# Attention scores of a graph network laid out by unit, head and node, and node sums by one selector for two heads

## The chip, the cores and the metric

The kernel runs on one core of one Trainium2 chip. The metric is the device time of a run in microseconds; three runs of the kernel before gave 3250.22, 3252.38 and 3263.53, median 3252.38 us.

## The reference

Two layers of a graph attention network (GATv2, two heads) over 3125 nodes of 128 features and 100000 edges sorted by their target node, each followed by a small MLP, then a residual and a layer norm. What matters here is the attention:

```python
xl = (h @ Wl + bl).reshape(n, 2, 128)
xr = (h @ Wr + br).reshape(n, 2, 128)
e = leaky_relu(xl[src] + xr[dst], 0.2)
score = einsum('ehd,hd->eh', e, att)
ex = exp(score - segment_max(score, dst)[dst])
out = segment_sum(xl[src] * (ex / (segment_sum(ex, dst)[dst] + 1e-16)), dst)
```

The kernel writes leaky_relu(z) as a linear part plus a multiple of relu(z). The linear part of the source node is one number per node and head, stored beside the row of the node.

## The kernel before, in words

The edges are cut into 391 units of 256 (K = 2 halves of 128 edges). A unit's targets lie in a window of W = 32 nodes. Two units (M = 2) are a step; a layer has 196 steps (NO; the last holds one unit) and some more for the tail. Each engine has a loop over the steps i written out by hand, in which every stage works on units of a fixed number of steps back; semaphores tie the engines together, and each engine keeps to its written order.

For a unit u the stages are:

- GpSimd gathers the 256 source rows (two indirect DMAs, L984; two heads, each 128 features, a one, and the linear part) into `rows`, a ring of 20 units. It does so for both units of a step after it has seen `z_ready` of the unit six before the first of them: the even unit of three steps back.
- SyncE loads the window's target rows (`xrw`, L1008) and the edges' positions (`relb`, L998, L1000).
- VectorE makes the one-hot matrix `oh` (L1330).
- TensorE's `project` (L1108, L1111) puts z = xl[src] + xr[dst] into a PSUM bank, transposed: four transposes and two bf16 matmuls of 256 columns; the last one increments `z_ready`.
- ScalarE takes the relu (`lz`, L1206). It waits for z and for `score_ready` of the step before.
- TensorE's `score` fills a 128x128 tile whose partitions are half, head and node of the window, its columns 128 edges: the linear part (L1083, four matmuls whose weights are one column of `rows` broadcast to 32 columns, the identity moving), the mask (L1086, two), and the relu part (L1092, four, after a wait for `lz_ready`). Outputs of 32 partitions use a strip of 32 columns of the array each. A float32 matmul of this kind is two matmul instructions with a weight load each. After the last one of a step: `score_ready`.
- ScalarE copies both tiles to `hold_s` (L1284); VectorE takes the smallest value of each partition (L1344), brings the two halves together (L1346, L1348), runs the minimum on over the units (L1352 to L1363) and writes `peak`; ScalarE takes the exponential, one instruction a unit (L1290); TensorE transposes it (L1197); ScalarE copies that to `wgt` (L1218).
- TensorE sums the weighted rows by node (L1181, four float32 matmuls a unit); VectorE adds them to a ring of accumulators (L1434).

In TensorE's step i the order is: sums of step i-6, score of the even unit of step i-1, projection of the even unit of step i, the transposes of the exponentials, score of the odd unit of step i-1, node work, projection of the odd unit of step i. From the minimum on, the units are taken as pairs that are shifted by one (`behind`): the odd unit of one step and the even one of the next.

Every eight steps a tile of 128 nodes is ready. Its node work is spread over the steps after: ScalarE copies nine accumulators to `stg`; TensorE adds up the groups of partitions and lays 32 nodes a group side by side (L1148, 24 instructions for each head, in two steps one after the other), then transposes, projection, MLP and, in the first layer, the next layer's projection (L1120 to L1165).

Of the kernel before, what the change touches and what calls it, by code (L numbers as in the profile page):

```python
# [59 lines left out]
assert NT % UT == 0 and N * UE == 8 * E and RING * 8 == P and K == 2 and RING % M == 0  # L60

def gnn(nc, x, src, dst, ln1_g, ln1_b, Wl, bl, Wr, br, att, gat_b, proj_W, proj_b, ln2_g, ln2_b, W1, b1,
# [9 lines left out]
    with ExitStack() as ctx:  # L73
# [11 lines left out]
        sel = sb("sel", [P, H, 3, W], F32)  # L85
# [97 lines left out]
def setup(nc, sb, sem, ps, wts, given, g):  # L183
# [68 lines left out]
    with nc.Block() as block:  # L252
# [31 lines left out]
        def _(pool):  # L284
# [26 lines left out]
            for t in range(K):  # L311
                for h in range(H):
                    o = t * HW + h * W
                    const(pool.affine_select(out=g["sel"][o:o + W, h, :, :], in_=g["sel"][o:o + W, h, :, :],
                                             compare_op=ALU.not_equal, fill=1.0, base=0, pattern=[[0, 3], [-1, W]],
                                             channel_multiplier=1))
            const(pool.memset(g["sel"][:, :, 0, S:W], 0.0))
            const(pool.memset(g["sel"][:, :, 2, 0:S], 0.0))
# [465 lines left out]
def behind(w):  # L784

    return [u for u in range(w * M - 1, w * M + M - 1) if 0 <= u < NU]

def behind_of(u):  # L790

    return (u + 1) // M

def node_step(t):

    return min(behind_of(t * TILE + 20), NO - 1) + 9

def edge_pass(nc, sb, sem, ps, wts, s, layer):
# [8 lines left out]
    lz_ready = sem("lz_ready")  # L810
    score_ready = sem("score_ready")
    held = sem("held")
    low_ready = sem("low_ready")
    low2_ready = sem("low2_ready")
# [68 lines left out]
    rows = sb("rows", [P, ROWS, K, H, RC], F32)  # L883
# [4 lines left out]
    hold_s = sb("hold_s", [P, 4 * M, P], F32)  # L888
    low = sb("low", [P, M], F32)
    low2 = sb("low2", [HW, M], F32)  # L890
    both = sb("both", [HW, M], F32)
    nxt = sb("nxt", [HW, M], F32)
    peak = sb("peak", [P, 4 * M], F32)
    ex = sb("ex", [P, 2 * M, P], F32)
    wgt = sb("wgt", [P, 2 * M, K * HW], F32)
# [46 lines left out]
    STEPS = NO + 7  # L942
# [32 lines left out]

    with nc.Block() as block:
        @block.gpsimd
        def _(pool):
            for u in range(NU):
                if u >= 3 * M and u % M == 0:  # L980
                    pool.wait_ge(z_ready, u - 3 * M + 1)
                for t in range(K):
                    c = u * K + t
                    pool.indirect_dma_start(rows[:, u % ROWS, t, :, :].rearrange("p h c -> p (h c)"), None,  # L984
# [608 lines left out]
```

## Time and profile before

| | |
|---|---|
| median of the timed runs | 3252.38 us |
| the profiled execution, first to last instruction (span) | 3186.6 us |
| what the median has beyond this span | 65.8 us |
| TensorE matmul busy | 2458.3 us (77%) |
| VectorE, ScalarE, GpSimd busy | 1438.1, 1377.3, 1539.2 us |
| mean granted clock of TensorE | 0.897 |

The page gives no other time of the profiled execution than its span. Busy times of TensorE are from records whose ends are modelled. An idle time in the views is put down to what released the engine; "issue" is a time in which the profile shows nothing that the engine waited for, and "remote" a releaser that it could not place.

### The profile page before, as it was taken

The numbers are of one execution on the slowest core, as the hardware profiler recorded it, in microseconds if no ns is written. First come the engines' busy times: TensorE is split into PE (matmuls) and PEld (weight loads), VectorE is DVE, ScalarE is ACT, GpSimd is POOL, SyncE is SP. The second block draws the span as 40 slices with busy tenths as digits, with TensorE's granted clock in tenths as the row PEclk, the third lists the DMA queues.
The fourth block names the chain that finished last, engine by engine and source line by source line (L and its number), as shares of the span: only waits on it lengthen the run. The fifth ranks groups of instructions, "written<-read, shape, count | busy, mean of one in ns | idle before, by whom it ended". The sixth has DMA issues, their size and how long they took to land. (4 is left out here: it accounts for less than half of the span.)

```text
span 3186.6 us, 87535 instructions
## 1 busy us (share of the span) xinstructions
PE 2458.3 (77%) x29581; PEld 1603.2 (50%) x29581; DVE 1438.1 (45%) x5714; ACT 1377.3 (43%) x3472; POOL 1539.2 (48%) x1664
## 2 busy tenths in 40 slices
PE   4678787878787787777758788777787788878775
PEld 2345555555555555555534455555455555545554
DVE  7334444444444444444543444444444443444444
ACT  4234444444444444444533444444444444444444
POOL 5655454554545454455225544455554454454440
PEclk7798999899989999999958998999999888899887
DMA  5443444444434444444224333343333333343330
GB/s 145 144 110 103 108 109 110 110 109 105 114 108 110 112 109 109 109 113 112 57 81 114 109 103 102 103 111 102 106 109 103 103 106 103 105 110 102 103 101 10
DMA packets 236833, 334.02 MB, mean 105 GB/s; under 512 B 51010, under 2 KB 160490, under 8 KB 236394
## 3 DMA queue, kind: packets, MB, share of 16 engines
q0 software_dynamic: 75072, 208.30, 24.9%
q1 hardware_dynamic: 161322, 120.16, 13.2%
q8 instruction: 240, 3.93, 0.5%
q14 instruction: 199, 1.63, 0.2%
HBM read 308.02 MB, written 20.25 MB: 103 GB/s over the span
## 5 line engine op out<-in xcount | busy, mean ns | idle before, releaser
L984 POOL DMA_INDIRECT rows<-table,src_t x1564 | 1488.2, 952 | 1449.6 <-PE psum L1111 1065.2
L1206 ACT ACTIVATE lz<-psum 128x512 f32<-128x512 f32 x782 | 467.1, 597 | 1632.3 <-DMA table<-row 543.2
L1092 PE MATMUL psum<-lz,att_w 128*32 128x128 f32 x6256 | 525.5, 307 | 315.2 <-issue 279.9
L1108 PE MATMUL psum<-ident,rows 128*128 128x128 f32 x3128 | 572.6, 308 | 71.6 <-issue 36.8
L1434 DVE SCALAR_TENSOR_TENSOR acc<-acc,keep,psum 128x129 f32 x782 | 273.3, 349 | 537.1 <-remote 322.4
L1108 PEld LDWEIGHTS psum<-ident,rows 128*128 128x128 f32 x3128 | 377.4, 154 | 258.2 <-issue 219.2
L1092 PEld LDWEIGHTS psum<-lz,att_w 128*32 128x32 f32 x6256 | 198.9, 113 | 491.9 <-issue 406.2
L1083 PE MATMUL psum<-ident,rows 128*32 128x128 f32 x6256 | 409.7, 302 | 35.1 <-issue 33.5
L1181 PE MATMUL psum<-rows,wgt 128*32 128x129 f32 x6256 | 317.2, 287 | 145.2 <-issue 98.8
L1330 DVE TENSOR_SCALAR oh<-relb,win_col,less 128x256 bf16<-128x256 int16 x782 | 247.6, 362 | 237.0 <-PE psum L1092 82.1
L1111 PE MATMUL psum<-oh,xrw 96*128 96x256 bf16 x1564 | 335.3, 297 | 6.6 <-DVE acc L1434 4.1
L1290 ACT ACTIVATE ex<-hold_s,peak 128x128 f32<-128x128 f32 x782 | 274.7, 405 | 84.7 <-DVE peak L1363 82.9
L1181 PEld LDWEIGHTS psum<-rows,wgt 128*32 128x32 f32 x6256 | 175.3, 111 | 269.1 <-issue 256.8
L1086 PE MATMUL psum<-oh,mask_w 128*64 128x128 bf16 x1564 | 218.8, 252 | 61.5 <-issue 60.0
L1083 PEld LDWEIGHTS psum<-ident,rows 128*32 128x32 f32 x6256 | 189.5, 114 | 136.4 <-issue 135.4
L1086 PEld LDWEIGHTS psum<-oh,mask_w 128*64 128x64 bf16 x1564 | 94.9, 110 | 232.1 <-issue 230.0
L1197 PE MATMUL psum<-ident,ex 128*128 128x128 f32 x782 | 176.7, 313 | 11.4 <-ACT wgt L1218 11.4
L1111 PEld LDWEIGHTS psum<-oh,xrw 96*128 96x128 bf16 x1564 | 167.8, 107 | 24.7 <-issue 8.7
L1344 DVE TENSOR_REDUCE low<-hold_s 128x2 f32<-128x256 f32 x392 | 162.2, 414 | 17.8 <-issue 13.0
L1148 PE MATMUL psum<-stg,sel 128*32 128x129 f32 x2400 | 159.8, 280 | 2.6 <-ACT stg L1301 1.7
L1148 PEld LDWEIGHTS psum<-stg,sel 128*32 128x32 f32 x2400 | 142.3, 111 | 6.4 <-ACT stg L1301 4.3
L1284 ACT COPY hold_s<-psum 128x256 f32<-128x256 f32 x392 | 143.6, 366 | 0.0
(256 smaller groups left out, 2169.5 us busy)
## 6 DMA issues: line engine op xcount, KB each, us to landing
xrw<-xr_split SPq DMA_DIRECT2D x782, 48.0 KB
relb<-rel_d SPq DMA_DIRECT2D x194, 192.0 KB
rows<-table,src_t POOLq DMA_INDIRECT x1564
relb<-cyc_d SPq DMA_DIRECT2D x194, 64.0 KB
xr_split<-split SPq DMA_DIRECT2D x50, 192.0 KB, 1.9
table<-row SPq DMA_DIRECT2D x50, 130.0 KB, 2.1
x_mid<-x SPq DMA_DIRECT2D x25, 64.0 KB
xo<-x_mid SPq DMA_DIRECT2D x25, 64.0 KB
```

Of the source, the lines that this page charges most:

```text
L984: pool.indirect_dma_start(rows[:, u % ROWS, t, :, :].rearrange("p h c -> p (h c)"), None, s["tables"][layer][0:NP, :], bass.IndirectOffset ...
L1083: pe.matmul(out[o:o + W, :], rows[:, u % ROWS, t, h, D + 1:RC].to_broadcast([P, W]), s["ident"][:, :], start=True, stop=False, skip_group_ ...
L1086: pe.matmul(out[t * HW:t * HW + HW, :], s["mask_w"][:, :], oh[:, u % (3 * M), t * P:t * P + P], start=False, stop=False, skip_group_check= ...
L1092: m = pe.matmul(out[o:o + W, :], w["att_w"][:, h * W:h * W + W], lz[:, u % M, h * UE + t * P:h * UE + t * P + P], start=False, stop=True, ...
L1108: pe.matmul(z[:, o:o + P], rows[:, u % ROWS, t, h, 0:D], s["ident"][:, :], is_transpose=True, start=(h == 0 and t == 0), stop=False, skip_ ...
L1111: m = pe.matmul(z[:, h * UE:h * UE + UE], xrw[:, place(u), h * D:h * D + D], oh[0:3 * W, u % (3 * M), :], start=False, stop=(h == H - 1), ...
L1148: mm = pe.matmul(bank(t)[m * W:m * W + W, h * (D + 1):h * (D + 1) + D + 1], s["sel"][:, h, c, :], stg[t % 2][:, 2 * m + c, :], start=(c == 0),
L1181: m = pe.matmul(sum_bank(i - 6)[o:o + W, c:c + D + 1], wgt[:, (u + 1) % (2 * M), o:o + W], rows[:, u % ROWS, t, h, 0:D + 1], start=True, s ...
L1206: act.activation(lz[:, u % M, :], ps[u % M][:, :], ACT.Relu).then_inc(lz_ready, 1)
L1290: m = act.activation(ex[:, (u + 1) % (2 * M), :], hold_s[:, place(u), :], ACT.Exp, bias=peak[:, place(u + 1):place(u + 1) + 1], scale=-1.0)
L1330: m = v.tensor_scalar(oh[:, u % (3 * M), :], relb[:, u % RING, :], s["win_col"][:, 0:1], s["less"][:, 0:1], ALU.is_equal, ALU.subtract)
L1434: m = v.scalar_tensor_tensor(a, a, s["keep"][:, u:u + 1], sum_bank(i - 7)[:, c:c + D + 1], ALU.mult, ALU.add)
```

## The change

A step's scores get one tile for both units. Before, a unit had a tile of its own: partitions were half, head and node, columns 128 edges. Now partitions are unit of the step, head and node (2 x 2 x 32), columns the unit's 256 edges.

- The linear part: ScalarE copies the one column per half, unit and head, broadcast to 32 columns, to a new tile `lin`, for both units at once; TensorE then needs two matmuls of 128 output partitions a step (before: eight of 32). ScalarE does this at the end of its step i for the units of step i, after it has waited for their rows.
- The mask: one matmul of 256 columns a unit (before: two of 128). The relu part: two of 256 columns (before: four of 128).
- `hold_s`, `ex` and `wgt` follow. The exponential is one instruction a step of 128x256 (before: two of 128x128). The minimum: a reduce over 256 columns, one copy of the second unit's 64 partitions; the operation that joined the halves is gone. `peak` is one column a step; the second unit's half is written a step later than the first's.
- The shift by one unit is gone (`behind` becomes `of_step`). Exponential, its transpose, `wgt`, sums and accumulation come one step later than before in the loops, which for the odd unit is the same place, and `node_step` grows by one.
- Node sums: the selector is laid out for both heads, so that a matmul gives 64 output partitions (two heads of 32 nodes): 12 instructions instead of 24 in each of the two steps. The copy to `gT` (L1241) reads the new order.

```diff
-    rows = sb("rows", [P, ROWS, K, H, RC], F32)
+    rows = sb("rows", [P, ROWS // M, K, M, H, RC], F32)
+    lin = sb("lin", [P, 2, K, M * HW], F32)
...
             def score(u):
                 g = u // M
-                out = scores(g)[:, u % M * P:u % M * P + P]
+                at = u % M * HW
+                out = scores(g)
                 if u % M == 0:
+                    n = len(of_step(g)) * HW
                     hold(pe, held, g - 1)
-                for t in range(K):
-                    for h in range(H):
-                        o = t * HW + h * W
-                        pe.matmul(out[o:o + W, :], rows[:, u % ROWS, t, h, D + 1:RC].to_broadcast([P, W]), s["ident"][:, :],
-                                  start=True, stop=False, skip_group_check=True)
-                for t in range(K):
-                    pe.matmul(out[t * HW:t * HW + HW, :], s["mask_w"][:, :], oh[:, u % (3 * M), t * P:t * P + P],
-                              start=False, stop=False, skip_group_check=True)
+                    pe.wait_ge(lin_ready, g + 1)
+                    for t in range(K):
+                        pe.matmul(out[0:n, t * P:t * P + P], lin[:, g % 2, t, 0:n], s["ident"][:, :],
+                                  start=(t == 0), stop=False, skip_group_check=True)
+                pe.matmul(out[at:at + HW, 0:UE], s["mask_w"][:, :], oh[:, u % (3 * M), :],
+                          start=False, stop=False, skip_group_check=True)
                 pe.wait_ge(lz_ready, u + 1)
-                for t in range(K):
-                    for h in range(H):
-                        o = t * HW + h * W
-                        m = pe.matmul(out[o:o + W, :], w["att_w"][:, h * W:h * W + W],
-                                      lz[:, u % M, h * UE + t * P:h * UE + t * P + P], start=False,
-                                      stop=True, skip_group_check=True)
+                for h in range(H):
+                    o = at + h * W
+                    m = pe.matmul(out[o:o + W, 0:UE], w["att_w"][:, h * W:h * W + W],
+                                  lz[:, u % M, h * UE:h * UE + UE], start=False, stop=True, skip_group_check=True)
...
-                        for m in range(P // W):
+                        for m in range(2):
                             for c in range(3):
-                                mm = pe.matmul(bank(t)[m * W:m * W + W, h * (D + 1):h * (D + 1) + D + 1],
-                                               s["sel"][:, h, c, :], stg[t % 2][:, 2 * m + c, :], start=(c == 0),
+                                mm = pe.matmul(bank(t)[m * HW:m * HW + HW, q * (D + 1):q * (D + 1) + D + 1],
+                                               s["sel"][:, c, :, :].rearrange("p h w -> p (h w)"),
+                                               stg[t % 2][:, 2 * (2 * q + m) + c, :], start=(c == 0),
                                                stop=(c == 2), skip_group_check=True)
...
+                new = of_step(i)
+                if new:
+                    for u in new:
+                        act.wait_ge(rows_in[u % ROWS], (u // ROWS + 1) * (16 * K))
+                    hold(act, score_ready, i - 1)
+                    act.copy(lin[:, i % 2, :, :].rearrange("p t (c w) -> p (t c) w", w=W),
+                             rows[:, ring(new[0]), :, :, :, D + 1:RC].rearrange("p t u h c -> p (t u h) c"
+                                                                                ).to_broadcast([P, K * M * H, W])
+                             ).then_inc(lin_ready, 1)
```

## Rows read from the trace of the kernel before

**Rows 1.** The page's span and busy times, and the core's granted clock.
```profile
span 3186.6 us, 87535 instructions
...
PE 2458.3 (77%) x29581; PEld 1603.2 (50%) x29581; DVE 1438.1 (45%) x5714; ACT 1377.3 (43%) x3472; POOL 1539.2 (48%) x1664
...
core 0: 3186.6 us, clock 0.897
```
**Rows 2.** Waits: engine and line, releaser, total us, times, longest us.
```profile
POOL rows L984 <- PE psum L1111: 1065.2, 374, 5.1
ACT lz L1206 <- remote: 512.1, 222, 13.5
...
POOL rows L984 <- issue: 363.3, 1179, 4.0
...
PE psum L1092 <- issue: 279.9, 496, 1.7
```
**Rows 3.** Timeline of one cycle: start us, us, engine, line, count, [idle before <- releaser].
```profile
1067.91 0.43 PE L1083 MATMUL psum<-ident,rows 128*32 128x128 f32 x8
1068.03 0.95 POOL L984 DMA_INDIRECT rows<-table,src_t  x1 [2.58 <-PE psum L1111]
...
1068.27 0.25 PE L1086 MATMUL psum<-oh,mask_w 128*64 128x128 bf16 x2
...
1068.44 0.43 PE L1092 MATMUL psum<-lz,att_w 128*32 128x128 f32 x8
...
1068.80 0.65 PE L1108 MATMUL psum<-ident,rows 128*128 128x128 f32 x4
...
1069.29 0.38 PE L1111 MATMUL psum<-oh,xrw 96*128 96x256 bf16 x2
...
1069.61 0.65 PE L1181 MATMUL psum<-rows,wgt 128*32 128x129 f32 x16
...
1071.79 0.95 POOL L984 DMA_INDIRECT rows<-table,src_t  x1 [0.30 <-issue]
1072.24 0.38 PE L1092 MATMUL psum<-lz,att_w 128*32 128x128 f32 x2 [0.51 <-issue]
1073.67 0.47 PE L1092 MATMUL psum<-lz,att_w 128*32 128x128 f32 x6 [1.05 <-issue]
1073.71 0.60 ACT L1206 ACTIVATE lz<-psum 128x512 f32<-128x512 f32 x1 [1.94 <-remote]
...
1074.07 0.66 PE L1108 MATMUL psum<-ident,rows 128*128 128x128 f32 x4
...
1074.57 0.38 PE L1111 MATMUL psum<-oh,xrw 96*128 96x256 bf16 x2
...
1075.22 0.94 POOL L984 DMA_INDIRECT rows<-table,src_t  x1 [2.48 <-PE psum L1111]
```
**Rows 4.** Timeline of TensorE near a layer's end, gathers done: two steps' sums.
```profile
3109.27 0.87 PE L1181 MATMUL psum<-rows,wgt 128*32 128x129 f32 x16
...
3114.48 0.65 PE L1181 MATMUL psum<-rows,wgt 128*32 128x129 f32 x16
```
**Rows 5.** Groups by line: count | busy us, mean ns of one | idle before.
```profile
L984 POOL DMA_INDIRECT rows<-table,src_t x1564 | 1488.2, 952 | 1449.6 <-PE psum L1111 1065.2 <-issue 363.3 <-remote 8.6
...
L1218 ACT COPY wgt<-psum 128x256 f32<-128x256 f32 x390 | 142.7, 366 | 0.0
...
L1148 PE MATMUL psum<-stg,sel 128*32 128x129 f32 x2400 | 159.8, 280 | 2.6 <-ACT stg L1301 1.7 <-DVE xrf L1492 0.9
```
**Rows 6.** Timeline of TensorE, three groups of instructions one after another.
```profile
1075.99 1.16 PE L1131 MATMUL psum<-h,w 128*128 128x128 f32 x8
...
1076.98 1.02 PE L1137 MATMUL psum<-wlr,h 128*128 128x512 f32 x2
...
1077.84 0.60 PE L1108 MATMUL psum<-ident,rows 128*128 128x128 f32 x4
```
**Rows 7.** The page's row of the DMA queue for one engine's instructions.
```profile
q8 instruction: 240, 3.93, 0.5%
```

More of the change, by code:

```diff
@@ L781, in of_step, with step_of @@
     return [u for u in range(w * M, w * M + M) if 0 <= u < NU]
[L784 to L792, printed above, removed]
+def step_of(u):
+    return u // M
 def node_step(t):
-    return min(behind_of(t * TILE + 20), NO - 1) + 9
+    return min(step_of(t * TILE + 20), NO - 1) + 10
 def edge_pass(nc, sb, sem, ps, wts, s, layer):
@@ L974, in place, with ring @@
         return u % (4 * M)
+    def ring(u):
+        return u // M % (ROWS // M)
     with nc.Block() as block:
@@ L983, in _ @@
                     c = u * K + t
[L984 removed]
+                    pool.indirect_dma_start(rows[:, ring(u), t, u % M, :, :].rearrange("p h c -> p (h c)"), None,
                                             s["tables"][layer][0:NP, :],
@@ L1107, in project @@
                         o = h * UE + t * P
-                        pe.matmul(z[:, o:o + P], rows[:, u % ROWS, t, h, 0:D], s["ident"][:, :], is_transpose=True,
+                        pe.matmul(z[:, o:o + P], rows[:, ring(u), t, u % M, h, 0:D], s["ident"][:, :], is_transpose=True,
                                   start=(h == 0 and t == 0), stop=False, skip_group_check=True)
@@ L1180, in _ @@
                                 o = t * HW + h * W
-                                m = pe.matmul(sum_bank(i - 6)[o:o + W, c:c + D + 1], wgt[:, (u + 1) % (2 * M), o:o + W],
-                                              rows[:, u % ROWS, t, h, 0:D + 1], start=True, stop=True)
+                                q = u % M * HW + h * W
+                                m = pe.matmul(sum_bank(i - 7)[o:o + W, c:c + D + 1], wgt[:, (i - 7) % 2, t, q:q + W],
+                                              rows[:, ring(u), t, u % M, h, 0:D + 1], start=True, stop=True)
                     m.then_inc(sums_ready, 1)
@@ L1190, in _ @@
                         project(i * M + j)
-                    old = behind(i - 4)
-                    if j == 0 and old:
-                        pe.wait_ge(ex_ready, i - 3)
-                        hold(pe, wgt_ready, i - 4)
-                        for u in old:
-                            c = (u + 1) % M * P
-                            m = pe.transpose(ps[4][:, c:c + P], ex[:, (u + 1) % (2 * M), :], s["ident"][:, :])
+                    if j == 0 and of_step(i - 5):
+                        pe.wait_ge(ex_ready, i - 4)
+                        hold(pe, wgt_ready, i - 5)
+                        for t in range(K):
+                            m = pe.transpose(ps[4][:, t * P:t * P + P], ex[:, (i - 5) % 2, t * P:t * P + P],
+                                             s["ident"][:, :])
                         m.then_inc(ex_turned, 1)
@@ L1279, in _ @@
                 if new:
[L1280 to L1281 removed]
+                    n = len(new) * HW
                     act.wait_ge(score_ready, i - 1)
[L1283 to L1293 removed]
+                    hold(act, ex_ready, i - 5)
+                    act.copy(hold_s[0:n, (i - 2) % 4, :], scores(i - 2)[0:n, 0:UE]).then_inc(held, 1)
+                old = of_step(i - 4)
+                if old:
+                    n, c = len(old) * HW, (i - 4) % 4
+                    act.wait_ge(max_ready, min(i - 2, NO))
+                    hold(act, ex_turned, i - 5)
+                    act.activation(ex[0:n, (i - 4) % 2, :], hold_s[0:n, c, :], ACT.Exp, bias=peak[0:n, c:c + 1],
+                                   scale=-1.0).then_inc(ex_ready, 1)
+                new = of_step(i)
[7 more added lines that the diff above has]
+                             ).then_inc(lin_ready, 1)
                 for t in nodes(i, -2):
[L1295 removed]
+                    act.wait_ge(added, min(step_of(t * TILE + 20), NO - 1) + 1)
                     hold(act, comb_ready, t - 1)
@@ L1334, in lowest @@
             def lowest(b):
-                new = of_step(b)
-                n, o = len(new), place(new[0])
+                n = len(of_step(b))
                 c = b % 8 * M + 1
```

105 lines of the change are left out of this document (43 added, 62 removed).

## The prediction

> **What bounds the kernel now.** I read the page's engine busy times, the waits, the timeline of one step with all engines, a stretch of it in which no gathers run, and the groups by line. TensorE is busy 77% and no other engine reaches half [rows 1]. So it looks like the bound, but its busy share hides how it loses time.
>
> The waits come next [rows 2]. GpSimd issues the gathers of a step (two units, four gathers) in one burst: 1179 gaps inside bursts of 363.3/1179 = 0.31 us, and 374 long waits for TensorE of 1065.2/374 = 2.85 us. With 952 ns for a gather [rows 5] a mean cycle is 4 x 0.952 + 3 x 0.31 + 2.85 = 7.58 us. The layers have 391 cycles, and nearly all of the time lies in them. ScalarE's relu waits 512.1 us on something the view calls remote, and TensorE sits 279.9 us in L1092 for no reason that the profile shows (issue).
>
> One cycle shows what both are [rows 3]. The burst starts at 1068.03 and its last gather at 1071.79 (ending 1072.74). TensorE runs freely at first: L1092, L1108, L1111, L1181 start 0.36, 0.49, 0.32 us apart. L1111 at 1069.29 lasts 0.38 us by its record and finishes z of the odd unit, yet the relu that waits for just this z starts at 1073.71, 4.0 us later and 0.97 us after the last gather ended. Meanwhile TensorE comes to a crawl: two matmuls of L1092 at 1072.24, then nothing until 1073.67, when everything moves at once. Then 6 matmuls of L1092, 4 of L1108 and 2 of L1111 finish z of the next even unit, and with it the next burst starts at 1075.22. So during a burst the engines hear late of what TensorE finished, and TensorE gets only a certain number of instructions past a finished but unreported one: from L1111 to the standstill these are 16 (L1181), 8 (L1083), 2 (L1086) and 2 (L1092), some 28 to 30 matmuls with their weight loads. The trace does not name the resource that is shared.
>
> The check is the end of a layer, where the gathers are over [rows 4]: a whole step, with L1131 in it, takes 3114.48 - 3109.27 = 5.21 us, with no standstill. Gathers cost TensorE over 2 us a step. The loop that sets the time is thus: z of the even unit, burst of 4.7 us, report 0.97 us after it, the matmuls that did not fit, z of the next even unit.
>
> **How many matmuls fit.** By the code a step has 66 matmul instructions outside the node work (fp32 counts two): L1181 16, L1083 16, L1086 4, L1092 16, L1108 8, L1111 4, L1197 2. Twelve of them come after the standstill [rows 3], so 54 fit between one even z and the report. After the change the lin matmuls are 4 for 16, the mask 2 for 4, the att matmuls 8 for 16: 44 in all, ten under 54. Node work adds 9 a step on average before ((29581 - 391 x 66)/391, less some preparation [rows 1]) and 6 after, since L1148's 2400 [rows 5] become 1200. The average step, 50, fits too; one with the 8 of L1131 does (52), one with 12 of L1148 is two over.
>
> A lower count could also be worth nothing: the instruction queue q8 moves 3.93 MB in 240 packets and takes 0.5% of the DMA engines [rows 7]. The Trainium skill's page "Runtime: NRT & Kernel Launch", section Instruction fetch mechanics, calls the crossing from one 16 KiB block of instructions to the next mostly hidden; by it fewer instructions save nothing by themselves, and the sum would be that of the first rival below. The row agrees that fetching is light, and says nothing on the standstill.
>
> **Part by part.** Durations are start to start, at full clock, a step.
> - lin (L1083): two groups of 8 at 0.36 us [rows 3] go. Four fp32 instructions over all 128 columns come: L1131's 8 take 0.99 us, so 0.12 each [rows 6], 0.50 together, perhaps 0.1 to refill. -0.72 + 0.55 = about -0.15.
> - mask (L1086): 2 x 0.17 us now [rows 3]. One of 256 columns for two of 128 that run side by side: L1111, two of 256 columns in 0.32, bounds one at 0.16 to 0.25. Between -0.02 and +0.16; I take +0.1.
> - att (L1092): this is what the change makes worse. Eight fp32 instructions in four column strips now take 0.36. An fp32 instruction of 512 columns takes 0.43 (L1137, two in 0.86 [rows 6]), so one of 128 takes 0.107; eight in a row would be 0.86, so they do run four at a time, 0.21 plus 0.15 fixed. The new four have 256 columns (0.215 each) in two strips: 0.43 + 0.15 = 0.58 a unit if the two strips overlap, 1.01 if they don't. So +0.44 a step, up to +1.3. I take +0.44, because the strips overlap in the present rows.
> - sums (L1181), transposes, L1111: same number and shapes. One more change between tile widths on the even unit, one less on the odd: nothing.
> - node sums (L1148): 24 of 32 columns for 12 of 64, twice in 8 steps. 24 rows of 280 ns mean overlap now; between half the time and all of it. At most -0.2 a step, I take -0.05.
> - ScalarE: a copy of 256 columns for lin, 0.37 us (as L1218 [rows 5]), comes, one exponential goes for a wider one. ScalarE is 43% busy [rows 1] and reads rows a step before TensorE needs lin, so it hides; it also waits for the gathers of step i at the end of its step i, with relus of the next step queued behind. Those rows were asked for three steps earlier. TensorE's new wait for lin stands before the even unit's mask and att matmuls and the next projection, so a late copy would hold all of them, and the next burst. I price it at 0, and at up to 0.3 us a step if it is late.
> - VectorE: one small operation of the running minimum goes, in a chain that is read a step later than before; the engine is 45% busy [rows 1], so 0.
> - The exponential, its transpose, the weights, the sums and the addition into acc are each a step later for the even unit. The ring of 10 steps of rows still holds: the sums of step i-7 come before the matmul whose report lets the gathers reuse that place. One short step more at each layer's end: +10 us in all.
>
> TensorE's own work thus goes from some 4.9 to 5.25 us a step (5.21 with L1131 in it [rows 4]). That is below the new cycle, but close to it.
>
> **The sum.** In the clean cycle, the next burst could start with the report instead of after 12 matmuls: 1075.22 - 1073.67 = 1.55 us shrinks to some 0.25, the cycle from 7.19 to 5.9. The mean cycle has node work, more columns and stretches at half clock (granted 0.897 on the mean [rows 1]): I give back 0.3 of the 1.3. The mean wait of 2.85 goes to 1.85, and 374 x 1.0 = 374 us fall away. The span goes from 3186.6 to 3186.6 - 374 + 10 = 2823; the runs' median is 3252.4, 65.8 above this span, and I keep that: 2889 us.
>
> **Rivals.**
> - *TensorE's columns decide (slower).* If the standstill is tied to the time under the burst and not to the number of instructions, the same stretch is lost and +0.35 us of columns is added at every step: 391 x 0.35 = 137, time 3252 + 137 + 10 = about 3400; with att strips that do not overlap, 391 x 1.2 = 470, 3730. For it: the release always follows the last gather, and the q8 instruction queue takes only 0.5% [rows 7], so fetching is no bandwidth matter. Against it: TensorE stops in the midst of L1092, between two matmuls that wait for nothing, which is a matter of count. It decides once 12 matmuls still lie after the report. Chance 0.11.
> - *A late relu takes the place.* The even z then waits on lz of the even unit, whose relu waits for a score report that is itself held. The cycle keeps 0.9 of the 1.3: saving 0.4 x 374 = 150, time 3110. For it: relus are the ones that wait for remote reports [rows 2]. Chance 0.20, of which 0.04 ends within 0.5%.
> - *The bursts join.* If z of the even unit is reported inside the burst, GpSimd needs only 4 x (0.952 + 0.31) = 5.05 us a step and TensorE's 5.25 to 5.6 us bounds: 7.58 - 5.6 = 2.0 x 391 = 780, time 2480. Against it: no report of an odd z comes inside this burst [rows 3]. Chance 0.07.
> - *The forecast*: 0.62, of which 0.01 ends within 0.5%.
>
> So 2889, and 2690 to 3260 for eight times in ten; the slower case is mostly left out. Within 0.5% (16 us, about what a measurement tells from none): 0.05. Slower: 0.11. Faster: 0.61 + 0.16 + 0.07 = 0.84.
>
> **What would show it.** Right: GpSimd's mean wait for TensorE falls from 2.85 toward 1.9 us; the next even z (L1111) has its record before the end of the burst, and the burst starts some 0.2 us after the report; L1092's issue idle nearly goes, while its work grows from 0.36 to 0.58 us a unit; matmul instructions fall from 29581 to about 19800 (391 x 22 + 1200 = 9800 fewer). Wrong: TensorE still stands still in the even unit's L1092 after fewer than 54 matmuls, or ScalarE's new copy stands before a late relu; or the granted clock falls well under 0.9 because TensorE idles more, which would double the 5.25 us where it does.

## The result, and the profile after

The changed kernel took 2737.89 us (median of 4 runs, 2737.19 to 2738.52) against 3252.69 us for the kernel before (4 runs): ratio 0.8414, 95% interval 0.8394 to 0.8434. Forecast were 2889 us within 2690 to 3260.

That result belongs to a condition that the experiments below found to come and go. In it TensorE's finished work is reported late (its semaphores are seen to rise long after the recorded end of the instruction that raises them) while gathers run, and the kernel before takes some 3250 us. In most of the later runs it was absent: the kernel before took 2207 to 2212 us, and this same change made it 4.5% slower. Both stand in this document; each ratio is against the kernel before, run beside it on the same chip.

The page of the changed kernel, rows as in [rows 1] and [rows 7]:

```profile
span 2736.0 us, 67939 instructions
...
PE 2284.2 (83%) x19785; PEld 1419.5 (52%) x19785; DVE 1318.3 (48%) x5318; ACT 1421.5 (52%) x3474; POOL 1547.2 (57%) x1664
...
q8 instruction: 165, 2.70, 0.4%
```

Its waits, as in [rows 2] (engine and line, releaser, total us, times, longest us). The gathers are now L980, z's last matmul is L1105, the relu L1201:

```profile
DVE acc L1431 <- remote: 859.3, 345, 5.4
ACT lz L1201 <- PE psum L1087: 551.1, 265, 3.5
POOL rows L980 <- issue: 363.5, 1180, 4.0
...
POOL rows L980 <- PE psum L1105: 293.5, 171, 3.5
...
POOL rows L980 <- DMA table<-row: 182.8, 116, 3.1
...
POOL rows L980 <- remote: 149.6, 96, 3.0
```

The gaps inside the bursts are what they were: 363.5/1180 = 0.31 us. The one kind of long wait has become three by name. In the code all three are the one wait for z, and the view names another releaser for 212 of them; a reader who looks only for L1105 would count 171 waits and miss 212. Together they are 293.5 + 182.8 + 149.6 = 625.9 us in 383 waits, 1.63 us each, against 2.85 [rows 2]. That is nearly the whole gain: 1065.2 + 8.6 [rows 5] - 625.9 = 447.9 us, and the span fell by 3186.6 - 2736.0 = 450.6.

One cycle of the changed kernel (start us, us, engine, line; as [rows 3]):

```profile
1007.11 0.38 PE L1105 MATMUL psum<-oh,xrw 96*128 96x256 bf16 x2
...
1007.43 0.65 PE L1177 MATMUL psum<-rows,wgt 128*32 128x129 f32 x16
...
1007.88 0.60 ACT L1201 ACTIVATE lz<-psum 128x512 f32<-128x512 f32 x1 [0.44 <-PE psum L1105]
1008.00 0.71 PE L1080 MATMUL psum<-ident,lin 128*128 128x128 f32 x4
...
1008.87 0.63 PE L1087 MATMUL psum<-lz,att_w 128*32 128x256 f32 x4
...
1009.43 0.66 PE L1102 MATMUL psum<-ident,rows 128*128 128x128 f32 x4
1009.50 0.95 POOL L980 DMA_INDIRECT rows<-table,src_t  x1 [0.30 <-issue]
...
1009.92 0.38 PE L1105 MATMUL psum<-oh,xrw 96*128 96x256 bf16 x2
...
1010.78 0.27 PE L1082 MATMUL psum<-oh,mask_w 128*64 128x256 bf16 x1 [0.25 <-issue]
...
1011.53 0.66 PE L1087 MATMUL psum<-lz,att_w 128*32 128x256 f32 x4 [0.48 <-issue]
1011.82 0.85 DVE L1431 SCALAR_TENSOR_TENSOR acc<-acc,keep,psum 128x129 f32 x2 [3.22 <-remote]
1012.09 0.95 POOL L980 DMA_INDIRECT rows<-table,src_t  x1 [1.64 <-remote]
```

The second L1105 finishes z of the even unit at 1010.30 by its record, the last gather of the burst ends at 1010.45, and the report comes with everything else at 1011.8. The next burst follows 0.27 us later. Before, z of the even unit was still 12 matmuls away when the report came [rows 3]; now it is 1.5 us old. The standstill has not gone: it has moved behind the even z, to L1082 and L1087 of the odd unit, where GpSimd doesn't wait for it. Not every report is late, either: the odd z of this cycle, recorded to end at 1007.49, releases its relu at 1007.88, in the midst of the burst.

The traces also keep the time of each semaphore update. Set beside the recorded end of the instruction that makes it (the last one before it), they say over a whole run what the cycle shows once:

| trace | TensorE's updates recorded | over 0.3 us late | of the even z's, over 0.3 us late |
|---|---|---|---|
| kernel before | 1925 | 1024 | 10 of 388 |
| changed kernel | 1788 | 1317 | 329 of 383 |
| changed kernel, fifth run below (2302 us) | 1915 | 0 | 0 of 385 |

(Some updates are missing from the traces; where the match would make one over 9 us late, it is left out.) Updates by ScalarE and VectorE come within 0.012 us of the recorded end in 95 of 100 cases in all three traces. So it is TensorE's reports that are late. Before the change the even z, on which the next burst waits, was not among the late ones: TensorE got to it only after the burst. Now it ends before the burst's last gather does in four steps of five, and only its report is late.

### The profile page after: what moved, and what is told of

It is laid out like the page before. It is cut to its first block and busy times, and to the rows that moved or that the text cites. A ratio compares the mean times of both kernels' runs of the same rounds, so it can differ in the third digit from the quotient of the medians.

```text
span 2736.0 us, 67939 instructions
## 1 busy us (share of the span) xinstructions
PE 2284.2 (83%) x19785; PEld 1419.5 (52%) x19785; DVE 1318.3 (48%) x5318; ACT 1421.5 (52%) x3474; POOL 1547.2 (57%) x1664
## 5 line engine op out<-in xcount | busy, mean ns | idle before, releaser
L980 POOL DMA_INDIRECT rows<-table,src_t x1564 | 1496.3, 957 | 993.3 <-issue 363.5
L1201 ACT ACTIVATE lz<-psum 128x512 f32<-128x512 f32 x782 | 470.0, 601 | 1105.0 <-PE psum L1087 551.1
L1431 DVE SCALAR_TENSOR_TENSOR acc<-acc,keep,psum 128x129 f32 x782 | 273.3, 349 | 956.3 <-remote 859.3
L1087 PE MATMUL psum<-lz,att_w 128*32 128x256 f32 x3128 | 564.7, 394 | 122.0 <-issue 101.9
L1102 PE MATMUL psum<-ident,rows 128*128 128x128 f32 x3128 | 537.0, 287 | 114.0 <-issue 78.4
L1102 PEld LDWEIGHTS psum<-ident,rows 128*128 128x128 f32 x3128 | 344.0, 142 | 399.9 <-issue 361.6
L1177 PE MATMUL psum<-rows,wgt 128*32 128x129 f32 x6256 | 257.1, 280 | 69.2 <-DVE acc L1431 66.1
L1105 PE MATMUL psum<-oh,xrw 96*128 96x256 bf16 x1564 | 303.7, 274 | 9.9 <-issue 9.9
L1080 PE MATMUL psum<-ident,lin 128*128 128x128 f32 x1568 | 280.8, 302 | 3.7 <-issue 3.7
L1087 PEld LDWEIGHTS psum<-lz,att_w 128*32 128x32 f32 x3128 | 135.4, 108 | 273.2 <-issue 166.1
L1080 PEld LDWEIGHTS psum<-ident,lin 128*128 128x128 f32 x1568 | 207.0, 192 | 82.2 <-issue 81.6
L1282 ACT ACTIVATE ex<-hold_s,peak 128x256 f32<-128x256 f32 x392 | 202.8, 517 | 78.0 <-issue 38.2
L1082 PE MATMUL psum<-oh,mask_w 128*64 128x256 bf16 x782 | 232.7, 298 | 11.3 <-issue 11.2
L1177 PEld LDWEIGHTS psum<-rows,wgt 128*32 128x32 f32 x6256 | 153.0, 109 | 151.4 <-issue 134.5
L1289 ACT COPY lin<-rows 128x256 f32<-128x256 f32 x392 | 156.1, 398 | 35.9 <-DMA rows<-table,src_t 32.6
L1342 DVE TENSOR_REDUCE low<-hold_s 128x1 f32<-128x256 f32 x392 | 162.4, 414 | 18.5 <-issue 11.1
L1105 PEld LDWEIGHTS psum<-oh,xrw 96*128 96x128 bf16 x1564 | 155.4, 100 | 27.1 <-issue 17.6
L1082 PEld LDWEIGHTS psum<-oh,mask_w 128*64 128x64 bf16 x782 | 83.2, 106 | 119.8 <-issue 73.5
L1210 ACT COPY wgt<-psum 128x256 f32<-128x256 f32 x392 | 143.5, 366 | 0.7 <-PE psum L1191 0.7
```

The costliest lines, as they stand in the source:

```text
L980: pool.indirect_dma_start(rows[:, ring(u), t, u % M, :, :].rearrange("p h c -> p (h c)"), None, s["tables"][layer][0:NP, :], bass.Indirect ...
L1080: pe.matmul(out[0:n, t * P:t * P + P], lin[:, g % 2, t, 0:n], s["ident"][:, :], start=(t == 0), stop=False, skip_group_check=True)
L1082: pe.matmul(out[at:at + HW, 0:UE], s["mask_w"][:, :], oh[:, u % (3 * M), :], start=False, stop=False, skip_group_check=True)
L1087: m = pe.matmul(out[o:o + W, 0:UE], w["att_w"][:, h * W:h * W + W], lz[:, u % M, h * UE:h * UE + UE], start=False, stop=True, skip_group_c ...
L1102: pe.matmul(z[:, o:o + P], rows[:, ring(u), t, u % M, h, 0:D], s["ident"][:, :], is_transpose=True, start=(h == 0 and t == 0), stop=False, ...
L1105: m = pe.matmul(z[:, h * UE:h * UE + UE], xrw[:, place(u), h * D:h * D + D], oh[0:3 * W, u % (3 * M), :], start=False, stop=(h == H - 1), ...
```

## The experiments

The kernel before was timed beside the experiments. It took 2209.1 us beside the first four, 2207.02 beside the fifth and sixth, 2209.34 beside the seventh and eighth, 3262.0 beside the ninth and tenth, and 2211.77 beside the last two. The expectations of the first four took the 3250 as their base; with the base gone their numbers could not be met.

**1 to 3: matmuls and columns added to the changed kernel.** The first makes the att matmuls narrower and twice as many, the second adds 24 one-column matmuls a step, the third four of 256 columns. The added ones of the second and third write beside the scores, but change them; the work behind them is the same.

```diff
 e1_att_split
-                for h in range(H):
-                    o = at + h * W
-                    m = pe.matmul(out[o:o + W, 0:UE], ...
+                for t in range(K):
+                    for h in range(H):
+                        o = at + h * W
+                        m = pe.matmul(out[o:o + W, t * P:t * P + P], ...
 e2_pad24 (12 a unit, after the mask)
+                for _ in range(12):
+                    pe.matmul(out[0:HW, 511:512], s["mask_w"][:, :], s["mask_w"][:, 0:1], start=True, stop=True, ...
 e3_wide4 (2 a unit, after the mask)
+                for _ in range(2):
+                    pe.matmul(out[0:HW, UE:2 * UE], s["mask_w"][:, :], oh[:, u % (3 * M), :], start=True, stop=True, ...
```

> The changed kernel with the relu part of a score in four matmuls of 128 columns again, as before the change, instead of two of 256: the same columns in the same two strips, but 8 matmul instructions more a step (52 outside the node work instead of 44). Count theory (TensorE gets about 54 matmul instructions past the even unit's z before it stands still): 52 fits, node steps of 60 and more do not, so 0 to +80 us, 2740 to 2820. Column theory (the new kernel is quicker for something else, and TensorE's time in columns decides): no change, 2738 within 10 us.

> The changed kernel with 24 more bf16 matmuls of a single column a step (12 ahead of each unit's relu part, into unused columns), 68 a step outside the node work, next to no columns. Count theory: some 14 to 20 matmuls too many a step lie after the report again, so the cycle goes from 6.37 us to 7.2 or more: +300 to +450 us, 3040 to 3190. Column theory: 24 single columns at 30 to 60 ns are 0.7 to 1.4 us of TensorE a step, of which its idle time hides most: below +150 us.

> The changed kernel with 4 more bf16 matmuls of 256 columns a step: 1024 columns or 0.43 us of array time, but only 4 instructions (48 outside the node work). Count theory: fits, at most +60 us where TensorE's own work (some 5.3 us of a 6.37 us cycle) becomes the bound. Column theory: +0.43 us x 391 = +168 us, 2906.

Measured, beside 2209.1 for the kernel before: 2309.14 us (ratio 1.0447, interval 1.043 to 1.0465), 2515.12 (1.1381, 1.1356 to 1.1406) and 2410.33 (1.0906, 1.0888 to 1.0924). Against the changed kernel itself, which the fifth run put at 2304.65 on another chip, the narrower att matmuls cost 4.5 us in all, no more than the kernel before differs from chip to chip, so eight more instructions in the same two strips are nothing. The 24 one-column ones cost (2515 - 2305)/391 = 0.54 us a step, 22 ns each (0.7 to 1.4 us was expected); the four wide ones (2410 - 2305)/391 = 0.27 us (0.43 was expected). Here TensorE is the bound and everything added to it shows. These runs say nothing on how many matmuls fit before a late report, which they were made for, since no report was late.

**4: the kernel before without its lin matmuls.** It leaves out L1083, and with it the linear part of the scores; the mask matmuls start the sum.

```diff
 e4_before_no_lin
-                    for h in range(H):
-                        o = t * HW + h * W
-                        pe.matmul(out[o:o + W, :], rows[:, u % ROWS, t, h, D + 1:RC].to_broadcast([P, W]), ...
```

> The kernel before without its L1083, so the linear part of the scores is left out (the mask matmul starts the sum): 16 matmul instructions and 0.7 us a step less, 50 instructions outside the node work; everything else as before. Count theory: 50 fits, the mean cycle falls from 7.6 us to about 6.4, saving 430 to 500 us, 2750 to 2820. Column theory: 0.7 us x 391 = 270 us, 2980.

Measured: 2206.51 us, ratio 0.9988 (0.9978 to 0.9997). Sixteen matmuls a step fewer, and nothing gained. The group of gathers of this run (count | busy us, mean ns | idle before) says what bounds:

```profile
L984 POOL DMA_INDIRECT rows<-table,src_t x1564 | 1491.3, 954 | 483.9 <-issue 464.7 <-PE psum L1106 15.2 <-POOLq L129 3.9
```

GpSimd waits 15.2 us for TensorE in the whole run, and issues one gather after another: (1491.3 + 483.9)/391 = 5.05 us a step. That is the floor of this kernel, as the third rival had worked it out.

**5: the changed kernel, once more, unedited.**

> The changed kernel itself, beside the kernel before on one chip, because in the runs e1 to e4 the kernel before took 2209 us and not 3252. Count theory, with late reports of TensorE's finished work as its condition: where the kernel before takes about 3250, the changed one takes about 2738 (ratio 0.84) and reports are late in its trace; where it takes about 2210, none are late, the count of instructions costs nothing, and the columns added (0.35 us a step) show: 2240 to 2300, ratio 1.01 to 1.04. Rival, that the change saves TensorE's time anywhere: faster on both.

Measured: 2304.65 us against 2207.02, ratio 1.0445 (1.0428 to 1.0463). The same two kernels, and the sign is turned. Its page, its gathers and two cycles of them:

```profile
PE 2150.1 (93%) x19785; PEld 1381.9 (60%) x19785; DVE 1321.5 (57%) x5318; ACT 1416.1 (62%) x3474; POOL 1557.6 (68%) x1664
...
L980 POOL DMA_INDIRECT rows<-table,src_t x1564 | 1505.6, 963 | 548.9 <-issue 442.4 <-PE psum L1105 102.6 <-POOLq L129 3.9
```
```profile
1005.75 0.95 POOL L980 DMA_INDIRECT rows<-table,src_t  x1 [0.30 <-issue]
...
1007.00 0.94 POOL L980 DMA_INDIRECT rows<-table,src_t  x1 [0.30 <-issue]
...
1008.17 0.38 PE L1105 MATMUL psum<-oh,xrw 96*128 96x256 bf16 x2
1008.83 1.25 POOL L980 DMA_INDIRECT rows<-table,src_t  x1 [0.89 <-PE psum L1105]
...
1010.38 0.94 POOL L980 DMA_INDIRECT rows<-table,src_t  x1 [0.30 <-issue]
```

The ratio lies just over the 1.04 that was expected for this case. z, recorded to end at 1008.55, starts a gather at 1008.83, 0.28 us later, and none of the 1915 recorded updates of TensorE is over 0.3 us late. Beside the first trace of the same kernel, the span is shorter by 2736.0 - 2300.8 = 435.2 us and the gathers' idle time by 993.3 - 548.9 = 444.4 us. TensorE is 93% busy and GpSimd waits for it now and then: the bound has gone from the gathers to TensorE.

**6 and 7: half the att columns.** The same edit in the kernel before (L1092, 64 of 128 columns) and in the changed one (128 of 256); the other half of the relu part is left out.

```diff
 e6_before_att_half
-                        m = pe.matmul(out[o:o + W, :], ..., lz[:, u % M, h * UE + t * P:h * UE + t * P + P], ...
+                        m = pe.matmul(out[o:o + W, 0:P // 2], ..., lz[:, u % M, h * UE + t * P:h * UE + t * P + P // 2], ...
 e7_after_att_half
-                    m = pe.matmul(out[o:o + W, 0:UE], ..., lz[:, u % M, h * UE:h * UE + UE], ...
+                    m = pe.matmul(out[o:o + W, 0:P], ..., lz[:, u % M, h * UE:h * UE + P], ...
```

> The kernel before with half of the columns of its L1092 (64 of 128, so the relu part is left out for half of the edges): the same number of instructions, 0.1 us of columns a group, 0.2 us a step less. With late reports (kernel before at 3250) the count theory expects within 30 us of the kernel before, the column theory 3170. Without them (2210) the gathers bound the kernel before (four of 0.95 us and four gaps of 0.31 a step), so no change either way: 2200 to 2212.

> The changed kernel with half of the columns of its relu-part matmuls (128 of 256, so the relu part is left out for half of the edges); instructions as in the changed kernel. Without late reports (kernel before at 2207): if the two column strips are what makes it slower, TensorE's step goes from 5.31 to 4.9 us and the four gathers a step (5.05 us) bound again: 2205 to 2225, ratio 1.00 to 1.01. If something else does (ScalarE's copy, the later pipeline), it stays near 2300. With late reports (3250): 2738 within 30 us, since the burst and not the columns sets the cycle.

Measured: 2206.87 us (ratio 0.9999, 0.9989 to 1.0009) and 2211.08 (1.0004, 0.9994 to 1.0014). In the kernel before the columns are hidden under the gathers; in the changed one the loss is gone with half of them, so it is TensorE's work that makes the loss. That it is just these columns the run doesn't show: anything that takes the 0.25 us a step by which TensorE is over the gathers would do as much. The two undisturbed steps under the tenth run price the parts.

**8: the parts of the change that keep the four strips.** The kernel before, with ScalarE's copy to `lin` and one full-width lin matmul a unit (2 instructions for 8), and with the 64-wide node sums; mask, att matmuls, exponential and the order of the steps as before. It has 54 matmul instructions a step beside the node work.

```diff
 e8_hybrid
-                for t in range(K):
-                    for h in range(H):
-                        o = t * HW + h * W
-                        pe.matmul(out[o:o + W, :], rows[:, u % ROWS, t, h, D + 1:RC].to_broadcast([P, W]), ...
+                    pe.wait_ge(lin_ready, g + 1)
+                pe.matmul(out[:, :], lin[:, g % 2, u % M, :], s["ident"][:, :], start=True, stop=False, ...
```

> The kernel before with only two parts of the change: the linear part as broadcast copies by ScalarE, in the layout of before (one fp32 matmul a unit), and the node sums of 64 partitions. The scores keep the layout with four strips: 54 matmul instructions a step outside the node work, fewer columns than before. Without late reports the gathers bound it as they bound the kernel before: 2200 to 2212, ratio 1.00; if ScalarE's copy is what costs, 2290 or more. With late reports (3250): about 6 instructions of an average step (60) are over the 54: cycle 6.7 to 7.0, 2860 to 2980.

Measured: 2207.84 us, ratio 0.9993 (0.9984 to 1.0003): the gathers bound it as they bound the kernel before, so it loses nothing where the change loses 4.5%. Its undisturbed step (L1182 at 499.73 to L1182 at 503.85 in its trace) is 4.12 us.

**9 and 10: half the gathers.** One gather a unit instead of two in both kernels, once the ring has been filled.

```diff
 e9_before_half_gathers, e10_after_half_gathers
-                for t in range(K):
+                for t in range(K if u < ROWS else 1):
```

> The kernel before with one gather a unit instead of two, once each of the 20 places of the ring has been filled (the second half of each later unit keeps the rows of the ring's first filling, so half of the source rows are left out; all other work is unchanged). It measures TensorE's own step of the kernel before, which its gathers hide where TensorE's reports come promptly. GpSimd's burst is then 2 x 0.95 + 0.31 = 2.2 us. Count and columns theories (prompt reports): TensorE's own work decides, between 4.7 and 5.0 us a step; 5.02 falls to that, time 2080 to 2200 beside 2207 for the kernel before. If the gathers load TensorE by themselves, beyond their own length, the step falls further, under 4.6 us. If this chip reports late and the kernel before takes about 3250: with bursts half as long the hold lasts about 2.2 + 0.97 us and the step falls to TensorE's own 5 us, time about 2250 to 2450; if the hold is tied to something else than the bursts, it stays over 2900.

> The changed kernel with the same edit (one gather a unit once the ring has been filled; the second halves keep old rows). Where reports come promptly it is bound by TensorE already (step 5.31 us, GpSimd waits for it), so both theories expect no or little change, 2230 to 2305; what it falls is what the gathers themselves cost TensorE. Its distance to the kernel before with half the gathers is the columns' own price: predicted 5.25 - 4.9 = 0.35 us a step, 130 to 180 us. If this chip reports late: also about 2300 to 2450, and then slower than the kernel before with half the gathers, which would show that the change loses wherever nothing is held.

Here the kernel before took 3262.0 us: the condition of the predicted pair was back. Measured: 2391.4 us (2 runs, ratio 0.7332, 0.7263 to 0.7401) and 2330.7 (2 runs, 0.7146, 0.7125 to 0.7166). So the hold is tied to the bursts: with bursts of 2.2 us for 4.7 the kernel before gets 870 us faster, 2.2 us a step. The second expectation was that the changed kernel would then be the slower one. That was wrong: it is still the faster by 61 us, and the traces show why. The kernel before with half the gathers, a held step and the free one after it:

```profile
490.92 0.65 PE L1181 MATMUL psum<-rows,wgt 128*32 128x129 f32 x16 [0.82 <-issue]
...
493.56 0.94 POOL L984 DMA_INDIRECT rows<-table,src_t  x1 [2.91 <-PE psum L1111]
...
494.81 0.96 POOL L984 DMA_INDIRECT rows<-table,src_t  x1 [0.30 <-issue]
494.82 0.38 PE L1111 MATMUL psum<-oh,xrw 96*128 96x256 bf16 x2
...
496.55 0.58 ACT L1206 ACTIVATE lz<-psum 128x512 f32<-128x512 f32 x1
497.06 0.65 PE L1181 MATMUL psum<-rows,wgt 128*32 128x129 f32 x16 [1.46 <-DVE acc L1434]
497.50 0.43 PE L1083 MATMUL psum<-ident,rows 128*32 128x128 f32 x8
497.86 0.25 PE L1086 MATMUL psum<-oh,mask_w 128*64 128x128 bf16 x2
498.03 0.43 PE L1092 MATMUL psum<-lz,att_w 128*32 128x128 f32 x8
498.39 0.66 PE L1108 MATMUL psum<-ident,rows 128*128 128x128 f32 x4
...
501.11 0.65 PE L1181 MATMUL psum<-rows,wgt 128*32 128x129 f32 x16
```

And the changed kernel with half the gathers, the step with the same work:

```profile
491.71 0.65 PE L1177 MATMUL psum<-rows,wgt 128*32 128x129 f32 x16
492.29 0.71 PE L1080 MATMUL psum<-ident,lin 128*128 128x128 f32 x4
492.94 0.30 PE L1082 MATMUL psum<-oh,mask_w 128*64 128x256 bf16 x1
493.16 0.62 PE L1087 MATMUL psum<-lz,att_w 128*32 128x256 f32 x4
493.72 0.66 PE L1102 MATMUL psum<-ident,rows 128*128 128x128 f32 x4
...
496.34 0.65 PE L1177 MATMUL psum<-rows,wgt 128*32 128x129 f32 x16
```

Undisturbed, the old step takes 501.11 - 497.06 = 4.05 us and the new one 496.34 - 491.71 = 4.63. But the old kernel has held steps among the free ones (490.92 to 497.06 is 6.14 us): z ends at 495.20, its relu starts at 496.55, 0.78 us after the last gather. In the changed kernel late reports are fewer (300 of 1700 recorded updates are over 0.3 us late, for 811 of 1948) and they hold no step up: (busy + idle of its gathers)/391 = (784.2 + 1292.0)/391 = 5.31 us a step, about what the fifth run has where nothing is late, (1505.6 + 548.9)/391 = 5.25. The kernel before has (786.7 + 1344.5)/391 = 5.45.

**11 and 12: the second and the eighth once more**, to have the padding and the hybrid where reports are late.

```diff
 e11_pad24_late: the edit of e2_pad24
 e12_hybrid_late: the edit of e8_hybrid
```

> The changed kernel with 24 one-column bf16 matmuls a step, as in the second experiment, sent again because the kernel before took 3262 us on the chip of the last runs, as in the pair that was predicted (if it takes 2207 here, this repeats the second experiment, ratio about 1.14). At 3250: count theory (TensorE gets a fixed number of matmuls, about 54 a step from even z to report, past an unreported one): 44 + 24 = 68 no longer fit, 14 are left after the report, the next burst waits for them and the gain is gone: mean wait of GpSimd back to 2.7 to 3 us, time 3150 to 3300. Columns theory (only TensorE's busy time counts, the 24 add 0.57 us by the second experiment): work of 5.3 + 0.57 = 5.9 us is still under the cycle of 6.4, time 2740 to 2960.

> The version of the eighth experiment (kernel before with lin copied by ScalarE and one matmul for it a unit, and 64-wide node sums; four column strips kept; 54 matmul instructions a step and 6 of node work), sent again where the kernel before takes about 3250. Count theory: 54 just fit, the steps with node work are a few over, so most of the gain comes: mean wait 1.7 to 2.1 us, time 2740 to 2950, near the changed kernel or between it and before. Columns theory: TensorE's own work is as before or 0.1 us less, so it would gain at most as the changed kernel loses by columns, and stay at 3150 to 3260. If the gain of the changed kernel comes from its layout in another way (the exponential or the shifted order), this one does not have it and stays over 3100.

Measured: 2509.18 us (2 runs, ratio 1.1353, 1.1307 to 1.1398) and 2208.98 (0.9988, 0.9977 to 0.9999), beside 2211.77 for the kernel before. It was the same chip as for the ninth and tenth, six minutes later, and the condition was gone: no recorded update of TensorE is over 0.3 us late in either trace. The runs repeat the second and eighth and leave open what those two edits do where reports are late.

## Why the prediction was right, and where its sizes were off

- **The bound (late reports tied to the bursts): right.** With half the gathers the kernel before falls from 3262 to 2391 us; where reports come promptly it takes 2207, and its gathers last as long (954 ns in the fourth run, 952 before). So of its 3252 us some 1045 are the hold. In the four traces of this condition 1024, 1317, 811 and 300 of TensorE's updates are late, in the ten others none. That the predicted pair ran in this condition was luck: the prediction took it for a trait of the kernel and nowhere asked whether it would last, and a pair in the other condition would have come out slower.
- **The even z comes before the report: right.** 1010.30 against 1011.8 in the cycle shown, and the burst follows 0.27 us after it (0.2 was named); over the run, 329 of 383 even z's have a late report where 10 of 388 had one.
- **"The release always follows the last gather": wrong in part.** The first rival leans on this. In the cycle of [rows 3] the relu of the even z starts within the burst, 0.37 us after the third gather began:

```profile
1070.91 0.60 ACT L1206 ACTIVATE lz<-psum 128x512 f32<-128x512 f32 x1 [3.01 <-remote]
```

  It had waited for the score of the step before, whose L1092 ends at 1068.87 [rows 3]; the update is recorded at 1070.83, 1.96 us late and yet inside the burst.
- **The mean wait: the first of the two mis-sized terms.** Forecast 1.85, measured 1.63 us. The clean cycle's gain of 1.3 was cut by 0.3 for node work, columns and clock. But the clock did not stay: granted 0.897 before [rows 1], 0.966 after. It goes with the condition: the kernel before itself was granted 0.879 to 0.886 where it took 3262 us and 0.961 to 0.970 where it took 2212. TensorE's instructions are quicker at it: the same z matmuls had a mean of 308 ns before (first row, L1108) and have 287 (second, L1102; count | busy us, mean ns | idle before):

```profile
L1108 PE MATMUL psum<-ident,rows 128*128 128x128 f32 x3128 | 572.6, 308 | 71.6 <-issue 36.8 <-DMA rows<-table,src_t 33.8
```
```profile
L1102 PE MATMUL psum<-ident,rows 128*128 128x128 f32 x3128 | 537.0, 287 | 114.0 <-issue 78.4 <-DMA rows<-table,src_t 34.1
```

  The prediction named only the danger of the clock falling. How much of the 0.22 us is the clock's no run parts from the rest. The saving of the span is 450.6 us where 374 - 10 = 364 was the sum: 87 us, of which the waits are 447.9 - 374 = 74; the 10 us for the layers' ends did not show.
- **The 65.8 us between span and median: the second.** It was carried over to the changed kernel, where the profiled run took 2737.67 us for a span of 2736.0, 1.7 us more. In every later run on record the time is 1.6 to 1.95 us over the span. So those 66 us were no overhead: the profiled execution of before must itself have been quicker than the timed runs, though its own time is not on record. 64 us of the error; with the 87 it makes up the 2889 - 2738 = 151.
- **TensorE's own work: forecast +0.35 us a step, measured +0.58 in a plain one.** From the two undisturbed steps above: lin 0.36 and 0.35 became 0.65 in all (-0.06; -0.15 forecast, though its terms, 0.50 and 0.1 for 0.72, give -0.12); mask 0.17 and 0.18 became 0.22 and 0.23 (+0.10; +0.10); att 0.36 and 0.36 became 0.56 and 0.56 (+0.40; +0.44). These hold. What was priced at nothing is the start of lin behind the sums: L1181 to L1083 was 0.44, L1177 to L1080 is 0.58 us, 0.14 more where weights of 128 columns follow those of 32. The hybrid, which has the same succession, has the same 0.58; the cause beyond that was not tested. The mean step of the changed kernel is 5.25 to 5.31 us, and 5.25 was forecast, by luck: it was added up as 4.9 + 0.35, and with +0.58 the old step comes to about 4.7 (an estimate: 5.31 - 0.58).
- **Column strips.** Taken one after another the att matmuls of a unit would need 0.86 us in either layout (the prediction's working). Four strips did them in 0.36, 2.4 times as fast; two strips in 0.56, 1.5 times. The same page of the Trainium skill, section Measured speedup vs the span model, has 2.38 for three column tiles. Here too a strip gives less than its full share.
- **ScalarE's copy to lin: right.** 398 ns a copy, forecast 370, and TensorE's L1080, which waits for it, has 3.7 us of idle time before it in the whole run, put down to issue. Rows of the changed kernel:

```profile
L1289 ACT COPY lin<-rows 128x256 f32<-128x256 f32 x392 | 156.1, 398 | 35.9 <-DMA rows<-table,src_t 32.6 <-issue 3.4
```
```profile
L1087 PE MATMUL psum<-lz,att_w 128*32 128x256 f32 x3128 | 564.7, 394 | 122.0 <-issue 101.9 <-ACT lz L1201 18.1
...
L1080 PE MATMUL psum<-ident,lin 128*128 128x128 f32 x1568 | 280.8, 302 | 3.7 <-issue 3.7
```

  Matmul instructions: 19785, forecast 19800. L1092's idle time went from 279.9 [rows 2] to 101.9 (L1087), not nearly to nothing.
- **The rivals.** "Columns decide" was priced at 3400 us on the ground of late reports. It did not happen there, but its mechanism is what decides without them: the gathers' floor of 5.05 us a step lies under the new mean step of 5.31 and over the old one (4.7 by the estimate above; the gathers hide it in the runs), and the result is 1.0445. The prediction's point from which it decides (12 matmuls after the report) was the wrong one; the right one is whether reports are held at all. "A late relu" and "the bursts join" did not come: the even z ends before the last gather in four steps of five, GpSimd still has its long wait in nearly each cycle (383 waits in 391), and the span fell by more than the clean sum.

Open: what TensorE's reports share with the gathers, and why the same kernel on the same chip is held at one time and not held six minutes later. Open too whether the hybrid keeps the gain where they are held; where they are not, it takes as long as the kernel before.

## What to carry to other kernels

When a stage waits for a report that comes only at the end of somebody else's burst, put the work whose report it is before that end. What counted here was not the length of the work but the number of instructions ahead of it: 31 matmuls past an unreported one, and no more. And before such a change is kept, ask what the loop's floor is without the hold: here it was 5.05 us a step of gathers, the change took TensorE past it, and a gain of 16% in one condition is a loss of 4.5% in the other. The gap between a profile's span and the timed median is not a constant to carry over: it was 65.8 us before and 1.9 after. Scaling it with the span would not have helped much either (65.8 x 2823/3186.6 = 58.3); a gap so much wider than in other runs says that the profile shows another execution than the timed ones.

## What the runs showed of the hardware

- The same kernel took 3262.0 us (3 runs, 3257.58 to 3265.52) and, on the same chip six minutes later, 2211.77 us (9 runs, 2205.99 to 2214.45). What differs in the traces is how late TensorE's finished work is seen. From z's recorded end to what it starts it is 0.28 us in the one condition (the fifth run); in the other it is 1.35 (the ninth), 1.79 (the changed kernel's even z) and 4.0 us [rows 3]. By the recorded updates, 1024 of 1925 are over 0.3 us late in the kernel before and none of 1915 in the fifth run, while those of ScalarE and VectorE come at once in both. The kernel before has no trace in the prompt condition.
- While its reports were late, TensorE started at most 31 more matmuls, each with its weight load, past one that was not yet reported, and then stood still (the traces before, after and of the ninth run).
- A gather of 128 rows holds GpSimd 0.95 us, with 0.31 us to the next: 1564 of them are a floor of 1564 x 1.26 = 1970 us for this kernel.
- 24 one-column matmuls with their weight loads cost 22 ns each where TensorE is the bound.
